# Routed experts of a two-layer transformer: the block loop pipelined one block deeper

## The chip, the cores and the metric

The kernel runs on one core of one Trainium2 chip. The metric is the device time of the whole program in microseconds (us); of the kernel before, three runs took 781.25, 782.66 and 784.82 us, median 782.66 us. The engines named below are TensorE (PE; its weight loads are PEld), VectorE (DVE), ScalarE (ACT), GpSimd (POOL) and SyncE (SP), which here only issues transfers. The profile is one execution, taken by the hardware profiler.

## The reference

The input x has 32 sequences of 128 tokens with 128 features; `ctx` holds 32 sequences of 77 context tokens. Two layers follow, each an attention to the context and a mixture of eight experts, of which every token uses two:

```
x = x + xattn0(layernorm(x), ctx)          # 16 heads, softmax over the 77 context tokens
x = x + moe0(layernorm(x))                 # 8 experts: (silu(x W1 + b1) * (x W2 + b2)) W3 + b3, 256 wide
x = x + xattn1(layernorm(x), ctx)          # linear attention: softmax over features of q and k
x = x + moe1(layernorm(x))                 # 8 experts: gelu(x W1 + b1) W2 + b2, 512 wide,
                                           # and the mean of 2 shared experts for every token
# top_k(router(x), 2) chooses the two experts; softmax of their two logits weighs them
```

All operands are 32-bit floats.

## The kernel before, in words

Layer 0 is attention (`attention0`), then the routed experts (`routed(0)`); layer 1 is attention with the shared experts woven into it (`attention1`), then `routed(1)`. Each routed stage is a loop over blocks of sorted rows, and the change concerns this loop alone.

While the attention of a layer runs, POOL scatters each token's normalized row twice (once for each chosen expert) into a table in HBM sorted by expert (`xs_sorted`, line 553). The table is then worked through in NB = 40 blocks for each layer, u = 0 to 39 in layer 0 and 40 to 79 in layer 1: 31 big ones of 256 rows (two tiles of 128) and 9 small ones of 128 rows, in the order ssss, then bbs five times, then big ones alone. Which expert a block belongs to is known only at run time: DVE computes it, and SP reads it from `e_i` to set the address of the transfer.

For each block the steps are these, in the names of the code:

- SP, `block_weights` (line 445): the expert's weights, 450 KB in layer 0 and 578 KB in layer 1, into one of NWB = 5 buffers `w_blk`. It waits until the outputs of block u - 5 have been added (`y_sum`). `block_rows` (line 457): the block's rows, 130 KB, into one of NXR = 8 buffers `xr`, AHEAD = 6 blocks in front. SP issues the transfers of all blocks in one order: weights of u + 5, rows of u + 6, weights of u + 6, and so on. In the preload it issues weights and rows in turn.
- PE, `turn_x` (through the helper at line 1355): transposes the rows into PSUM bank 6.
- DVE, `copy_x` (line 1011): copies bank 6 into `xT`, of which there are two.
- PE, `up` (through the helper at line 1352): four products with the weights into two of the banks 0 to 3 (a block uses banks 2k and 2k + 1 with k = u % 2). It waits for `xT_ready`, for the weights, and until the hidden values of block u - 2 have left these banks (`h_ready`).
- Layer 0: ACT applies silu (line 797, into `hg`), then DVE, `gated`, multiplies (line 1019, into `hT`). Layer 1: ACT applies gelu (line 801, into `hT`).
- PE, `down` (line 1640): the second product into bank 4 or 5.
- DVE, `outputs`: adds the bias (line 1028, this is `y_sum`) and scales by the gate (line 1032). POOL, `results` (line 626): scatters the tiles back to token order in HBM (`y_tok`), one indirect transfer for each tile.

PE's order in iteration u is turn_x(u + 1), up(u), down(u - 1). DVE's is copy_x(u + 1), outputs(u - 2), gated(u) in layer 0, and for the first 24 blocks of layer 0 a third of `context_soft`, which belongs to the attention of layer 1.

When all blocks are done, SP reads the token-ordered results back (line 498), DVE adds them to x (line 1058), and in layer 1 ACT stores x.

## Time and profile before

| what | value |
|---|---|
| three runs | 781.25, 782.66, 784.82 us, median 782.66 us |
| the profiled execution | 784.91 us, of which the span of its instructions is 782.9 us |
| PE busy | 688.5 us, 88% of the span |
| DVE, POOL, ACT busy | 465.7, 381.2, 327.3 us |
| mean granted TensorE clock | 0.942 of full speed |
| bytes moved | 91.34 MB, mean 117 GB/s |

The profile's page cuts the span into 40 slices of 19.6 us and gives the busy share of each engine in tenths. Layer 0's routed blocks lie in slices 15 to 21 (about 280 to 409 us), layer 1's in slices 32 to 39 (from 623 us; the last matmul ends at 765 us). A row of a timeline reads: start, duration, engine, line, operation, output <- inputs, shapes, how many are merged, and in brackets how long the engine had been idle and what ended that. "remote" as a releaser means that the profile could not say which instruction sent the signal. Ends of matmuls are modelled, so the time of a stage of PE is best read from start to start.

### The profile page before, as it was taken

The page shows a single profiled execution, that of the slowest core. Times are in us where ns is not written, and L with a number is a line of the kernel's source. Part 1 is how long each engine was busy: PE and PEld are TensorE (multiplying, and loading weights), DVE is VectorE, ACT ScalarE, POOL GpSimd, SP SyncE. Part 2 cuts the span into 40 slices and gives each one's busy share as a digit, 9 for nine tenths or more (in the row PEclk, how much of TensorE's full clock was granted, in tenths as well). Part 3 has the DMA queues.
Part 4 walks back from the last instruction along what each step waited for, and adds up shares of the span by engine and source line. Part 5 has one row for each costly group of instructions (what it writes and reads, how often), then busy time and mean ns, then how long its engine had stood idle before and what let it go on. Part 6 is the DMA issues. An engine that isn't in the chain of part 4 may idle for free.

```text
span 782.9 us, 15683 instructions
## 1 busy us (share of the span) xinstructions
PE 688.5 (88%) x5118; PEld 510.3 (65%) x5118; DVE 465.7 (59%) x1347; ACT 327.3 (42%) x689; POOL 381.2 (49%) x502
## 2 busy tenths in 40 slices
PE   4999999999898968889878799999999689999990
PEld 2666666566666657878766545555554389999990
DVE  2566877787677667676656667676653523324326
ACT  2344455445333232222212456667764244444440
POOL 5213176566537524555551365555555414454452
PEclk9999999999889789999997899999999979999996
DMA  6811111221101457776756000000000478877769
GB/s 164 258 12 10 10 28 26 30 30 25 32 12 35 126 166 237 215 225 204 212 165 173 0 18 21 28 29 21 24 28 27 123 234 258 270 238 246 227 196 285
DMA packets 102120, 91.34 MB, mean 117 GB/s; under 512 B 52953, under 2 KB 85849, under 8 KB 101721
## 3 DMA queue, kind: packets, MB, share of 16 engines
q1 hardware_dynamic: 86375, 68.80, 32.4%
q0 software_dynamic: 8640, 17.84, 6.4%
q10 hardware_dynamic: 7025, 3.70, 1.9%
q8 instruction: 42, 0.69, 0.4%
q14 instruction: 38, 0.30, 0.1%
HBM read 69.13 MB, written 22.72 MB: 117 GB/s over the span
## 4 chain that ended last, share of the span: by engine, by line
PE 53%; DVE 18%; issue 8%; DMA 5%; POOL 4%; ACT 4%; SPq 4%; another core or an unknown queue 3%; POOLq 0%; DVEq 0%; ACTq 0%
PE pair L1352 27%; PE pair L1640 10%; PE pair L1355 8%; DVE sm L1116 3%; DVE smax L1112 3%; POOL xs_sorted L553 2%; DMA xr<-xs_sorted 2%; PE pair L1458 2%; PE pair L1692 2%; PE pair L1473 2%; ACT xa L663 2%; DMA y_tok<-ysb,xr 1%; DMA xa<-y_tok 1%; DVE bns L1062 1%
## 5 line engine op out<-in xcount | busy, mean ns | idle before, releaser
L626 POOL DMA_INDIRECT y_tok<-ysb,xr x142 | 137.6, 969 | 145.5 <-DVE ysb L1032 116.3
L553 POOL DMA_INDIRECT xs_sorted<-xa,slot_i x128 | 130.2, 1017 | 93.5 <-DVE slot_i L939 59.0
L1352 PE MATMUL pair<-xT,w_all 128*128 128x256 f32 (+1 forms) x640 | 142.9, 369 | 0.0
L1640 PE MATMUL pair<-w_all,hT 128*128 128x128 f32 x852 | 110.8, 279 | 10.1 <-DVE hT L1019 10.0
L1352 PEld LDWEIGHTS pair<-xT,w_all 128*128 128x128 f32 x640 | 112.6, 201 | 10.4
L1640 PEld LDWEIGHTS pair<-w_all,hT 128*128 128x128 f32 x852 | 108.1, 195 | 15.1 <-issue 12.0
L801 ACT ACTIVATE hT<-pair,w_all 128x256 f32<-128x256 f32 (+1 forms) x160 | 62.0, 448 | 78.6 <-PE pair L1352 78.1
L1011 DVE COPY xT<-pair 128x256 f32<-128x256 f32 (+1 forms) x80 | 31.5, 394 | 104.9 <-PE pair L1355 88.7
L797 ACT ACTIVATE hg<-pair,w_all 128x256 f32<-128x256 f32 (+1 forms) x80 | 31.7, 447 | 93.5 <-PE pair L1352 68.3
L1112 DVE TENSOR_REDUCE smax<-pair 128x8 f32<-128x616 f32 x64 | 50.5, 788 | 33.2 <-PE pair L1352 32.8
L1352 PE MATMUL pair<-xeT_all,w_sh 128*128 128x512 f32 x128 | 69.2, 623 | 0.0
L818 ACT ACTIVATE hS<-pair,w_sh 128x512 f32<-128x512 f32 x64 | 43.9, 686 | 53.5 <-PE pair L1352 43.2
L1692 PE MATMUL pair<-hS,w_sh 128*128 128x512 f32 x128 | 65.4, 593 | 0.0
L1355 PEld LDWEIGHTS pair<-cst,sm 128*128 128x128 f32 x320 | 37.2, 151 | 26.4 <-issue 26.4
L1355 PE MATMUL pair<-cst,sm 128*128 128x128 f32 x320 | 52.8, 300 | 0.2 <-issue 0.2
L1116 DVE TENSOR_TENSOR sm<-pair,smax 128x616 f32<-128x616 f32 x64 | 51.2, 799 | 2.2
L1352 PE MATMUL pair<-hT,yS 32*128 32x308 f32 x192 | 41.8, 514 | 11.6 <-DVE sm L1116 10.0
L1355 PE MATMUL pair<-cst,xr 128*128 128x128 f32 x142 | 30.7, 288 | 18.7 <-DMA xr<-xs_sorted 7.0
L1019 DVE SCALAR_TENSOR_TENSOR hT<-pair,w_all,hg 128x256 f32<-128x256 f32 (+1 forms) x80 | 32.6, 448 | 24.2 <-remote 15.1
L701 ACT ACTIVATE wide<-pair 128x384 f32<-128x384 f32 x64 | 24.5, 434 | 44.5 <-PE pair L1355 44.5
L701 ACT ACTIVATE hS<-pair 128x384 f32<-128x384 f32 x64 | 24.6, 433 | 34.3 <-PE pair L1355 34.3
L1692 PEld LDWEIGHTS pair<-hS,w_sh 128*128 128x128 f32 x128 | 23.0, 190 | 23.7 <-issue 21.2
(194 smaller groups left out, 1100.5 us busy)
## 6 DMA issues: line engine op xcount, KB each, us to landing
w_all<-in_w SPq DMA_DIRECT2D x40, 578.0 KB
w_all<-in_w SPq DMA_DIRECT2D x40, 450.0 KB
xa<-y_tok SPq DMA_DIRECT2D x32, 256.0 KB, 5.6
xr<-xs_sorted SPq DMA_DIRECT2D x62, 130.0 KB
y_tok<-ysb,xr POOLq DMA_INDIRECT x142
xs_sorted<-xa,slot_i POOLq DMA_INDIRECT x128
out<-x_sb ACTq DMA_DIRECT2D x8, 256.0 KB, 3.1
xs_sorted<-in_pads SPq DMA_DIRECT2D x12, 130.0 KB, 4.3
```

The lines of the kernel that those rows point to most:

```text
L553: g.indirect_dma_start(xs_dram[l], bass.IndirectOffsetOnAxis(ap=slot_i[:, i:i + 1], axis=0), xa[:, GT * c + j // TOPK, j % TOPK, :], None) ...
L626: g.indirect_dma_start(y_dram[l], bass.IndirectOffsetOnAxis(ap=xr[u % NXR][:, t, P:P + 1].bitcast(I32), axis=0), ysb[u % NYB][:, t, :], None)\
L701: s_.activation(pT[T % 2][gr][:, 0:n], bank[2 + gr % 2][:, 0:n], ACT.Exp, scale=SCALE)\
L801: s_.activation(hT[k][:, c, 0:n], src, ACT.Gelu, bias=w[:, bcol + c:bcol + c + 1])\
L818: s_.activation(hS[i % 4][:], bank[4 + i % 2][:], ACT.Gelu, bias=w_sh[:, col:col + 1])\
L1019: v.scalar_tensor_tensor(hT[k][:, c, 0:n], chunk(bank[2 * k + 1], c, BLK)[:, 0:n], w[:, bcol + c:bcol + c + 1], hg[k][:, c, 0:n], ALU.add, ...
L1112: link(v.reduce_max(smax[ab][:].rearrange("q (b h) -> q b h", b=2), score(ab), AX.X))
L1116: v.tensor_tensor(sm[ab][:, 0:SPAN].rearrange("q (b h k) -> q b h k", b=2, k=NK), score(ab), smax[ab][:].rearrange("q (b h) -> q b h", b=2 ...
L1352: return mm(out_, l_, r_, start=True, stop=True)
L1355: return nc.tensor.transpose(out_, in_, ident)
L1640: last = mm(bank[4 + k][:, t * P:(t + 1) * P], hT[k][:, c, t * P:(t + 1) * P], chunk(w, nu + c, P), start=(c == 0), stop=(c == nc_ - 1))
L1692: mm(bank[6][:], w_sh[:, wd:wd + P], hS[i % 4][:], start=(c == 0), stop=(c == NC1S - 1))\
```

## The change

Buffers: six for weights instead of five, twelve for rows instead of eight, three each for `xT`, `hg`, `hT` instead of two. Rows are loaded 8 blocks ahead instead of 6. The room comes from `early`, one region that layer 0's attention uses first (`sm`, `kf4`, `rden`, `rdx`, `lent`) and the routed blocks afterwards. Rows are transposed two blocks ahead, into bank 6 or 7 in turn, and `down` runs two blocks back. On DVE `gated` comes one iteration later and stands before `outputs`, and `outputs` comes one later. Four row buffers count on the semaphores of the first inputs (`rows_in`), and one semaphore of ACT goes.

```diff
-NWB = 5
-NXR = 8
-AHEAD = NXR - 2
+NWB = 6
+NXR = 12
+AHEAD = 8
+DEEP = 3
...
-        w_all = sb("w_all", [P, NWB * WMAX])
-        w_blk = [w_all[:, i * WMAX:(i + 1) * WMAX] for i in range(NWB)]
+        early = sb("early", [P, 4300])
+        w_all = sb("w_all", [P, (NWB - 1) * WMAX])
+        w_blk = [w_all[:, i * WMAX:(i + 1) * WMAX] for i in range(NWB - 1)] + [early[:, 0:WMAX]]
...
+        def rows_in(u):
+
+            i = u % NXR
+            if i < 8:
+                return f"xr_in{i}", 16 * (u // NXR)
+            return f"x_in{i - 8}", 16 * (u // NXR + 1)
...
 (ACT, routed: up)
-                            after(act, S("h_ready"), NC0 * (u - 2) + c + 1)
-                            s_.activation(hg[k][:, c, 0:n], src, ACT.Silu, bias=w[:, bcol + c:bcol + c + 1])\
+                            after(act, S("h_ready"), NC0 * (u - DEEP) + c + 1)
+                            s_.activation(hg[u % DEEP][:, c, 0:n], src, ACT.Silu, bias=w[:, bcol + c:bcol + c + 1])\
...
 (DVE, routed)
                 def copy_x(u):
                     dve.wait_ge(S("xT_done"), u + 1)
-                    after(dve, S("up_done"), 2 * (u - 1))
+                    after(dve, S("up_done"), 2 * (u - DEEP + 1))
                     n = tiles_of(u) * P
-                    v.tensor_copy(xT[u % 2][:, 0:n], bank[6][:, 0:n]).then_inc(S("xT_ready"), 1)
+                    v.tensor_copy(xT[u % DEEP][:, 0:n], bank[6 + u % 2][:, 0:n]).then_inc(S("xT_ready"), 1)
...
                 copy_x(u0)
-                for u in range(u0, u1 + 2):
-                    if u + 1 < u1:
-                        copy_x(u + 1)
-                    if u >= u0 + 2:
-                        outputs(u - 2)
-                    if u < u1 and l == 0:
-                        gated(u)
+                copy_x(u0 + 1)
+                for u in range(u0, u1 + 3):
+                    if u + 2 < u1:
+                        copy_x(u + 2)
+                    if u0 < u <= u1 and l == 0:
+                        gated(u - 1)
+                    if u >= u0 + 3:
+                        outputs(u - 3)
...
 (PE, routed)
                 def turn_x(u):
-                    pe.wait_ge(S(f"xr_in{u % NXR}"), 16 * (u // NXR + 1))
-                    after(pe, S("xT_ready"), u)
+                    name, earlier = rows_in(u)
+                    pe.wait_ge(S(name), earlier + 16)
+                    after(pe, S("xT_ready"), u - 1)
                     for t in range(tiles_of(u)):
-                        last = turn(bank[6][:, t * P:(t + 1) * P], xr[u % NXR][:, t, 0:P])
+                        last = turn(bank[6 + u % 2][:, t * P:(t + 1) * P], xr[u % NXR][:, t, 0:P])
...
                 turn_x(u0)
-                for u in range(u0, u1 + 1):
-                    if u + 1 < u1:
-                        turn_x(u + 1)
+                if l == 1:
+                    pe.wait_ge(S("sx_added"), NGRP)
+                turn_x(u0 + 1)
+                for u in range(u0, u1 + 2):
+                    if u + 2 < u1:
+                        turn_x(u + 2)
                     if u < u1:
                         up(u)
-                    if u > u0:
-                        down(u - 1)
+                    if u > u0 + 1:
+                        down(u - 2)
```

The waits of `up` (`xT_ready` of u, the weights, `h_ready` of block u - 2) stay as they were.

PE, the start of layer 1's blocks. `cst,yS` is the last transpose of the shared experts, `cst,xr` is turn_x, `xT,w_all` is up, `w_all,hT` is down; in the changed kernel some buffers bear the name `early`. Before:

```order
L1355 MATMUL pair<-cst,yS 128x128 x4
L1355 MATMUL pair<-cst,xr 128x128 x2
L1352 MATMUL pair<-xT,w_all 128x128 x4
L1355 MATMUL pair<-cst,xr 128x128
L1352 MATMUL pair<-xT,w_all 128x128 x4
L1640 MATMUL pair<-w_all,hT 128x128 x4
L1355 MATMUL pair<-cst,xr 128x128
```

Changed:

```order
L1366 MATMUL pair<-cst,yS 128x128 x4
L1366 MATMUL pair<-cst,xr 128x128 x3
L1363 MATMUL pair<-xT,w_all 128x128 x4
L1366 MATMUL pair<-cst,xr 128x128
L1363 MATMUL pair<-early 128x128 x4
L1366 MATMUL pair<-cst,early 128x128 x2
L1363 MATMUL pair<-xT,w_all 128x128 x4
L1652 MATMUL pair<-w_all,hT 128x128 x4
```

Three blocks are transposed before the first up instead of two, and the first down comes after the third up instead of the second.

DVE, two blocks late in layer 0, where nothing else is woven in (`xT<-pair` is copy_x, `ysb` are the two operations of outputs, `hT<-pair,w_all,hg` is gated). Before:

```order
L1011 COPY xT<-pair 128x256
L1028 TENSOR_TENSOR ysb<-pair,w_all 128x256
L1032 TENSOR_TENSOR ysb<-ysb,xr 128x256
L1019 SCALAR_TENSOR_TENSOR hT<-pair,w_all,hg 128x256 x2
L1011 COPY xT<-pair 128x256
L1028 TENSOR_TENSOR ysb<-pair,w_all 128x256
```

Changed:

```order
L1021 COPY xT<-pair 128x256
L1029 SCALAR_TENSOR_TENSOR hT<-pair,w_all,hg 128x256 x2
L1038 TENSOR_TENSOR ysb<-pair,w_all 128x256
L1042 TENSOR_TENSOR ysb<-ysb,xr 128x256
L1021 COPY xT<-pair 128x256
L1029 SCALAR_TENSOR_TENSOR hT<-pair,w_all,hg 128x256 x2
```

The gated product now stands between the copy and the outputs of its iteration.

## Rows read from the trace of the kernel before

**Rows 1.** The page: its head, and granted clock in 40 slices.

```profile
span 782.9 us, 15683 instructions
...
PEclk9999999999889789999997899999999979999996
```

**Rows 2.** Busy time by stretch (busy us, instructions), then clock, DMA share, GB/s.

```profile
280.00:409.00 129.00, 111.58 (x677) 100.63 (x678) 87.26 (x229) 32.64 (x81) 65.41 (x68) 0.95 0.68 203
622.00:643.00 21.00, 15.24 (x89) 14.08 (x90) 4.79 (x16) 6.47 (x20) 2.97 (x4) 0.76 0.74 216
643.00:762.00 119.00, 119.00 (x848) 112.89 (x847) 39.29 (x107) 55.00 (x139) 60.43 (x63) 1.00 0.78 239
```

**Rows 3.** Waits, 265 to 420 us: who for whom, total, times, longest.

```profile
PE pair L1640 <- DVE hT L1019: 10.0, 5, 2.7
PE pair L1355 <- DVE xT L1011: 4.5, 4, 1.4
PE pair L1355 <- DMA xr<-xs_sorted: 2.4, 4, 1.6
```

**Rows 4.** Timeline of layer 0, one block and the stall behind it.

```profile
378.27 0.38 PE L1355 MATMUL pair<-cst,xr 128*128 128x128 f32 x2
...
381.11 0.38 PE L1355 MATMUL pair<-cst,xr 128*128 128x128 f32 x2
...
381.32 1.89 PE L1352 MATMUL pair<-xT,w_all 128*128 128x256 f32 x8
...
383.05 1.05 PE L1640 MATMUL pair<-w_all,hT 128*128 128x128 f32 x8
...
384.95 0.42 DVE L1011 COPY xT<-pair 128x256 f32<-128x256 f32 x1 [3.41 <-remote]
...
385.29 0.41 DVE L1028 TENSOR_TENSOR ysb<-pair,w_all 128x256 f32<-128x256 f32 x1
...
385.52 0.41 PE L1355 MATMUL pair<-cst,xr 128*128 128x128 f32 x2 [1.42 <-DVE xT L1011]
...
386.08 0.87 DVE L1019 SCALAR_TENSOR_TENSOR hT<-pair,w_all,hg 128x256 f32<-128x256 f32 x2
```

**Rows 5.** Timeline of PE in the middle of layer 1's blocks.

```profile
718.70 0.38 PE L1355 MATMUL pair<-cst,xr 128*128 128x128 f32 x2
...
720.64 1.95 PE L1640 MATMUL pair<-w_all,hT 128*128 128x128 f32 x16
722.43 0.38 PE L1355 MATMUL pair<-cst,xr 128*128 128x128 f32 x2
```

**Rows 6.** Timeline of SP's queue at the start of layer 1's blocks.

```profile
627.17 0.33 SPq L457 DMA_DIRECT2D xr<-xs_sorted  x1
628.27 0.33 SPq L445 DMA_DIRECT2D w_all<-in_w  x1
629.91 0.33 SPq L457 DMA_DIRECT2D xr<-xs_sorted  x1
...
632.68 1.99 SPq L457 DMA_DIRECT2D xr<-xs_sorted  x2
```

**Rows 7.** Timeline of PE there.

```profile
626.77 0.48 PE L1355 MATMUL pair<-cst,xr 128*128 128x128 f32 x1 [2.62 <-DMA xr<-xs_sorted]
...
629.56 0.48 PE L1355 MATMUL pair<-cst,xr 128*128 128x128 f32 x1 [0.60 <-DMA xr<-xs_sorted]
...
641.98 0.33 PE L1355 MATMUL pair<-cst,xr 128*128 128x128 f32 x1 [1.31 <-DMA xr<-xs_sorted]
642.15 1.90 PE L1352 MATMUL pair<-xT,w_all 128*128 128x256 f32 x8
```

**Rows 8.** Timeline of the end: the last two down products, POOL's scatters of blocks 78 and 79.

```profile
761.47 3.73 PE L1640 MATMUL pair<-w_all,hT 128*128 128x128 f32 x32
...
765.33 0.96 POOL L626 DMA_INDIRECT y_tok<-ysb,xr  x1 [2.00 <-DVE ysb L1032]
...
767.87 0.96 POOL L626 DMA_INDIRECT y_tok<-ysb,xr  x1 [0.30 <-issue]
```

More of the change, by code:

```diff
@@ L262, in build @@
         smax = [sb(f"smax{i}", [P, 2 * HG]) for i in range(2)]
-        sm = [sb(f"sm{i}", [P, NCK * P]) for i in range(2)]
-        kf4 = sb("kf4", [P, GT * NK])
-        rden = sb("rden", [P, P])
-        rdx = sb("rdx", [P, GT * P])
+        sm = [early[:, i * NCK * P:(i + 1) * NCK * P] for i in range(2)]
+        kf4 = early[:, 3328:3328 + GT * NK]
+        rden = early[:, 4148:4148 + P]
+        rdx = early[:, 3636:3636 + GT * P]
         cxm = sb("cxm", [P, 3, GT * H])
-        lent = [sb(f"lent{i}", [P, 1024])[:] for i in range(2)]
+        lent = [early[:, 1280 + i * 1024:1280 + (i + 1) * 1024] for i in range(2)]
         lg = sb("lg", [P, NT, E])
@@ L309, in build @@
         below = sb("below", [1, len(SETS), NYB * NQ])
[L312 to L315 removed]
+        xr = [sb(f"xr{i}", [P, 2, ROW]) for i in range(8)] + \
+             [early[:, 3072 + i * 2 * ROW:3072 + (i + 1) * 2 * ROW].rearrange("p (t d) -> p t d", t=2) for i in range(NXR - 8)]
+        xT = [sb(f"xT{i}", [P, BLK]) for i in range(2)] + [early[:, 2816:2816 + BLK]]
+        hg = [sb(f"hg{i}", [P, NC0, BLK]) for i in range(2)] + [early[:, 2304:2304 + NC0 * BLK].rearrange("p (c n) -> p c n", c=NC0)]
+        hT = [sb(f"hT{i}", [P, NC1, BLK]) for i in range(2)] + [early[:, 1280:1280 + NC1 * BLK].rearrange("p (c n) -> p c n", c=NC1)]
         ysb = [sb(f"ysb{i}", [P, 2, P]) for i in range(NYB)]
@@ L655, in _ @@
             act.wait_ge(S("pool_const"), 8)
-            s_.activation(table[:], ones_row[:, 0:1], ACT.Exp).then_inc(S("table"), 1)
+            s_.activation(table[:], ones_row[:, 0:1], ACT.Exp)
             act.wait_ge(S("head_in"), 16)
@@ L1017, in gated @@
                         dve.wait_ge(S("up_done"), 2 * u + 2)
-                        after(dve, S("down_done"), u - 1)
-                        v.scalar_tensor_tensor(hT[k][:, c, 0:n], chunk(bank[2 * k + 1], c, BLK)[:, 0:n],
-                                               w[:, bcol + c:bcol + c + 1], hg[k][:, c, 0:n], ALU.add, ALU.mult)\
+                        after(dve, S("down_done"), u - DEEP + 1)
+                        v.scalar_tensor_tensor(hT[u % DEEP][:, c, 0:n], chunk(bank[2 * k + 1], c, BLK)[:, 0:n],
+                                               w[:, bcol + c:bcol + c + 1], hg[u % DEEP][:, c, 0:n], ALU.add, ALU.mult)\
                             .then_inc(S("h_ready"), 1)
@@ L1629, in up @@
                     for c in range(nu):
-                        last = one(chunk(bank[2 * k + c // 2], c % 2, BLK)[:, 0:n], chunk(w, c, P), xT[k][:, 0:n])
+                        last = one(chunk(bank[2 * k + c // 2], c % 2, BLK)[:, 0:n], chunk(w, c, P), xT[u % DEEP][:, 0:n])
                         if c % 2 == 1:
@@ L1639, in down @@
                         for c in range(nc_):
-                            last = mm(bank[4 + k][:, t * P:(t + 1) * P], hT[k][:, c, t * P:(t + 1) * P],
+                            last = mm(bank[4 + u % 2][:, t * P:(t + 1) * P], hT[u % DEEP][:, c, t * P:(t + 1) * P],
                                       chunk(w, nu + c, P), start=(c == 0), stop=(c == nc_ - 1))
```

12 lines of the change are left out of this document (4 added, 8 removed).

## The prediction

> **What bounds the kernel now.** I read the page first: 782.9 us of span with a clock that falls below full speed in some slices [rows 1]. The change acts only in the two loops over routed blocks, so I cut these out by stretches of time. Layer 0's blocks take 129 us, in which PE is busy 111.6 us; the DMA engines are busy 68%, DVE 87.3 us [rows 2]. Layer 1's blocks fall in two parts: a start of 21 us with PE busy for only 15.2 us at a mean clock of 0.76, and then 119 us in which PE is busy for all 119.0 us at full clock [rows 2]. So in the body of layer 1 PE itself is the bound. There a block takes 722.43 - 718.70 = 3.73 us from turn to turn with nothing in between [rows 5], and no amount of buffering shortens it. What more buffering can win lies in layer 0 and at the two starts.
>
> In layer 0 the list of waits says what PE lacks: 10.0 us in five waits before `down` for the gated product, 4.5 us in four waits before `turn_x` for the copy of the previous block, 2.4 us in four for rows from HBM [rows 3]. A block that runs without a gap takes 381.11 - 378.27 = 2.84 us: turn 0.21, up 1.73 (383.05 - 381.32), down the remaining 0.90 [rows 4].
>
> The timeline of one stall shows what kind of wait it is. PE's transpose at 381.11 is over by 381.5, DVE has nothing to do, and yet its copy starts only at 384.95, after 3.41 us of idle time whose releaser the profile can't name. Meanwhile PE goes on with up and down until about 383.95 (381.11 + 2.84), then runs dry; the next transpose starts at 385.52, 1.57 us late [rows 4]. So signals from PE reach DVE late now and then, by more than the loop has in hand. The rows don't say why. The question is how much delay the new loop bears, and at which signal.
>
> **The change part by part.** The number of instructions on PE, DVE, ACT, POOL and SP is the same for every block; only order and distance change. So each term is a change of idle time on PE, or at the ends.
>
> *Waits for the gated product.* Before, gated(u) is needed by down(u), which follows down(u - 1), turn_x and up(u + 1) after up(u): 0.90 + 0.21 + 1.73 = 2.84 us of cover. After, down(u) is two blocks back, but up(u + 2) writes the banks that gated(u) reads and still waits for it. It comes 0.90 + 0.21 = 1.11 us later than the place where PE waited before. Against that, DVE now has the copy of block u + 3 in front of gated(u), 0.42 us [rows 4]. Net 0.69 us for each of the five waits: 3.4 us gained. Bounds: all 10.0 us gained (no late signal finds the loop short), and nothing gained. I take 3.4, since the bank rule is in the code and the distances are from rows.
>
> *Waits for the copy.* Before, a late signal of the transpose costs from the moment PE runs dry (2.84 us after the transpose started) to release + copy. After, PE goes on into the next transpose, 0.21 us more, and then stands before up(u + 1), which needs gated(u - 1), which on DVE stands behind the late copy. So the price becomes release + copy + gated, and gated takes 0.87 us [rows 4]: 0.87 - 0.21 = 0.66 us more for each of four waits, 2.6 us lost. Bounds: 4.5 us gained if these delays no longer matter, 2.6 us lost. I take the loss, as the stall in [rows 4] begins at exactly this signal.
>
> *Lead of the transfers.* SP may load weights when outputs of an old block are added. Before, outputs(u) runs in DVE's iteration u + 2 and the weights go to block u + 5; after, in iteration u + 3 for block u + 6: three iterations both times. Rows likewise, u + 6 turned in iteration u + 5, and u + 8 turned in iteration u + 6. The sixth and the twelve buffers only carry the deeper loop. But outputs now stand behind gated, 0.87 us later in their iteration [rows 4], so every transfer has 0.87 us less. PE waited for rows four times in layer 0 [rows 3]; the loss lies between nothing and, if one block in three of 40 falls short, 13 x 0.87 = 11.3 us. I take one such delay, 0.9 us lost, nearest to the small wait of 2.4 us that the trace has.
>
> *The start of layer 1.* PE transposes two ahead, so up(40) waits for the rows of block 42 instead of 41: these are in at 629.56 instead of 626.77 [rows 7]. The start is paced by SP, which spends 629.91 - 627.17 = 2.74 us for a pair of rows and weights, of which 1.10 us goes from rows to weights and 1.64 from weights to rows [rows 6]. Rows of blocks 44 and 45 were issued back to back from 632.68; now the sixth weights go between them, and rows of 46 and 47 follow at once, by my count issued at 632.68, 635.4, 637.1 and 638.7 with weights at 633.8. With 629.56 - 627.17 = 2.4 us from issue to transpose the rows of 47 are in at about 641.1. In between PE does up(43), down(41), up(44), down(42) and is at up(45) at about 642.9, where before it was at 642.15 [rows 7]; but before, down(43) was done by then, a small one of half of 1.79 us (720.64 to 722.43 [rows 5]). So 0.75 + 0.9 = 1.6 us lost, which the saturated body can't give back. Bounds: 0.9 (only the deferred product) and 3.0 (the rows of 46 take the 4.3 us that they took before). The new wait on `sx_added` has nothing behind it but this loop and is met before the rows of 41 arrive. The start of layer 0 is like it but waits longer for other things; by the same count its first big blocks come out even, 0.
>
> *The ends.* The last three down products of a layer now run back to back. In layer 1 a down takes 1.79 us [rows 5], but POOL takes 767.87 - 765.33 = 2.54 us to scatter a block [rows 8]. Before, two ran back to back and block 79's scatter waited on POOL for block 78; now 77, 78 and 79 queue up: 2.54 - 1.79 = 0.75 us later. Bounds 0 and 1.5. In layer 0 the same happens, but down(38) now covers part of the wait before down(39), which is among the five.
>
> The sum against the profiled execution: 784.91 - 3.4 + 2.6 + 0.9 + 1.6 + 0.75 = 787.4 us. The median of the runs is 2.25 us under the profiled time, so 785.1 us is what I forecast for the median, 2.4 us (0.3%) over 782.66. A difference below 0.5% (3.9 us) can't be told from no change here.
>
> **The rivals.**
>
> *The delays are absorbed.* The waits of PE for DVE in layer 0, 14.5 us [rows 3], mostly vanish. For it: the gaps come again and again, and the loop has one buffer more of each kind. The Trainium skill speaks for this: its page "Perfetto Trace Analysis", section on identifying performance opportunities, says that the same gap repeating on the engine that should be full can mean that there are too few buffers for the next tile. By that rule alone the 14.5 us would go. Against it stands that banks 0 to 3 still hold only two blocks, and that the copy now carries the gated product behind it. With all gone and start and end as above: 784.91 - 14.5 + 1.6 + 0.75 = 772.8, in the median 770.5; with two thirds gone, 775.3. Faster.
>
> *The lead runs short.* Outputs 0.87 us later shift weights and rows of every block. When PE runs at 2.84 us a block, three iterations are 8.5 us; from this about 1.1 us went before for turn, copy and first output, and 2.0 go now, so 6.5 us remain for SP, transfer and signal. If that fails for a third of the blocks: 784.91 - 3.4 + 2.6 + 11.3 + 1.6 + 0.75 = 797.8, median 795.5. For it: the DMA engines already move 239 GB/s in layer 1 and 203 in layer 0 [rows 2], with rows waited for four times. Against it: the waits for rows are 2.4 us in all. It decides once rows land less than 0.9 us before their turn. Slower; with half of it, 790.
>
> *Nothing moves.* The bank rule caps the loop at two blocks as before and the late signals find the same gap; only start and end count: 784.91 + 2.4, median 785.0. This gives the same number as the forecast and goes with it.
>
> **How the numbers follow.** Forecast with its neighbour "nothing moves": 0.40. Absorbed, wholly or in part: 0.31. Lead short, or late signals that cost more than I count: 0.29. The forecast's own range is 781 to 789: of it about a tenth lies over 786.6, and the two rivals reach into the band within 0.5% with a few in a hundred each. That gives faster by over 0.5% 0.31, within 0.5% 0.36, slower 0.33. For 8 in 10, I go down to 771, where all of the 14.5 us is gone, and up to 794, near the short lead in full.
>
> **What would show it.** In layer 0 the group of waits of `down` for the gated product should be gone and PE should wait before `up` instead, for the gated product, in total some 7 us of the old and 4 x 2.2 us for late copies. In a stall like that of [rows 4], DVE should run copy, gated, outputs in a row and PE start up after the gated product. Layer 0's blocks should take 128 to 131 us. In layer 1 the first up should start near 629.8 on the old clock of the trace instead of 627.04, and the body should still be 3.73 us a block with PE full. POOL's last scatter should start about 0.75 us later after the last down. The forecast is wrong if layer 0's blocks take under 124 us (delays absorbed), or if waits for `xr<-xs_sorted` or for weights grow beyond 6 us there (lead short).

## The result: 1.1% slower, and the profile after

The changed kernel took 790.78 us (median of 20 runs) beside 781.58 us for the kernel before (20 runs on the same chip): 1.0106 of its time, 95% interval 1.0085 to 1.0127, or some 8.3 us more. That ratio leaves out one slow run of the changed kernel (796.1 us), and the medians alone lie 9.2 us apart. The forecast was 0.3% more, no change that can be told.

The page and the stretches of the changed kernel, which answer to [rows 1, 2] (layer 0's blocks, the start of layer 1's, their body; us busy, then clock, DMA share, GB/s):

```profile
span 789.1 us, 15679 instructions
...
PEclk8699999998998779999996799999999879999995
...
279.80:406.30 126.50, 110.70 (x673) 98.95 (x672) 84.76 (x226) 32.19 (x81) 64.47 (x65) 0.97 0.68 207
626.50:648.00 21.50, 15.18 (x85) 13.65 (x86) 4.20 (x14) 7.40 (x22) 2.41 (x3) 0.68 0.74 221
648.00:769.90 121.90, 121.81 (x876) 115.63 (x874) 40.17 (x110) 55.32 (x138) 61.83 (x65) 1.00 0.79 242
```

The body of layer 1 is full as before. PE's waits from 265 to 420 us, which answer to [rows 3] (L1363 is the up products, L1366 the transposes, L1652 the down products):

```profile
PE pair L1363 <- DVE hT L1029: 8.7, 8, 2.2
...
PE pair L1366 <- DMA xr<-xs_sorted: 2.3, 4, 1.3
PE pair L1366 <- DMA early<-xs_sorted: 2.1, 4, 1.0
PE pair L1652 <- DVE ysb L1038: 2.0, 2, 1.5
...
PE pair L1366 <- DVE xT L1021: 0.3, 1, 0.3
```

No wait of a down product for the gated product is left; it is the up products that wait for it, 8.7 us where the old two groups had 14.5. Waits for rows rose from 2.4 to 4.4 us, and two waits for a bank of outputs came to 2.0. A stall like that of [rows 4]:

```profile
352.52 0.42 DVE L1021 COPY xT<-pair 128x256 f32<-128x256 f32 x1 [2.82 <-remote]
...
352.73 0.44 PE L1366 MATMUL pair<-cst,xr 128*128 128x128 f32 x2 [1.28 <-DMA xr<-xs_sorted]
352.86 0.87 DVE L1029 SCALAR_TENSOR_TENSOR hT<-pair,w_all,hg 128x256 f32<-128x256 f32 x2
353.64 0.41 DVE L1038 TENSOR_TENSOR ysb<-pair,w_all 128x256 f32<-128x256 f32 x1
353.87 1.97 PE L1363 MATMUL pair<-early,w_all 128*128 128x256 f32 x8 [0.70 <-DVE hT L1029]
```

Copy, gated product and outputs stand in a row behind the late signal, and the up product starts when the gated product is done, as forecast.

Layer 1's start and PE's block there, and the last scatter, which answer to [rows 5 to 8]:

```profile
626.54 0.45 PE L1366 MATMUL pair<-cst,xr 128*128 128x128 f32 x1 [2.14 <-issue]
630.42 0.45 PE L1366 MATMUL pair<-cst,xr 128*128 128x128 f32 x1 [3.43 <-DMA xr<-xs_sorted]
632.57 0.47 PE L1366 MATMUL pair<-cst,xr 128*128 128x128 f32 x1 [1.70 <-DMA xr<-xs_sorted]
632.84 1.49 PE L1363 MATMUL pair<-xT,w_all 128*128 128x128 f32 x6
...
721.73 0.38 PE L1366 MATMUL pair<-cst,early 128*128 128x128 f32 x2
...
725.46 0.38 PE L1366 MATMUL pair<-cst,early 128*128 128x128 f32 x2
...
766.07 3.74 PE L1652 MATMUL pair<-w_all,hT 128*128 128x128 f32 x32
...
773.07 1.03 POOL L636 DMA_INDIRECT y_tok<-ysb,xr  x1 [0.30 <-issue]
```

and the first transpose of the kernel before:

```profile
623.85 0.30 PE L1355 MATMUL pair<-cst,xr 128*128 128x128 f32 x1 [1.22 <-issue]
```

From first transpose to first up product it was 627.04 - 623.85 = 3.19 us and is 632.84 - 626.54 = 6.30. A block is still 725.46 - 721.73 = 3.73 us. The last block's scatter (the first of its two transfers) begins 773.07 - 769.81 = 3.26 us behind the last down product (2.66 before).

Cut at these marks, in us of the two profiled executions:

| stretch | before | after | difference |
|---|---|---|---|
| to layer 0's first up product | 280.44 | 279.87 | -0.6 |
| layer 0's blocks | 127.7 | 126.3 | -1.4 |
| last down product to layer 1's first transpose | 215.7 | 220.3 | +4.6 |
| first transpose to first up product | 3.2 | 6.3 | +3.1 |
| layer 1's blocks | 138.2 | 137.0 | -1.2 |
| last down product to the end | 17.7 | 19.3 | +1.6 |

That is the 6.2 us between the two spans. The largest term lies in a stretch whose own order of work the change does not touch.

### The profile page after: what moved, and what is told of

Read it like the earlier page. It is cut to its first block, busy times and chain, and to the rows that moved or that the text cites. A ratio compares the mean times of both kernels' runs of the same rounds, so it can differ in the third digit from the quotient of the medians.

```text
span 789.1 us, 15679 instructions
## 1 busy us (share of the span) xinstructions
PE 689.3 (87%) x5118; PEld 508.4 (64%) x5118; DVE 465.0 (59%) x1347; ACT 327.9 (42%) x689; POOL 382.1 (48%) x502
## 4 chain that ended last, share of the span: by engine, by line
PE 53%; DVE 17%; issue 10%; SPq 6%; DMA 5%; POOL 5%; ACT 4%; POOLq 0%; DVEq 0%; ACTq 0%
PE pair L1363 28%; PE pair L1652 10%; PE pair L1366 8%; DVE early L1127 3%; DVE smax L1123 3%; POOL xs_sorted L563 2%; PE pair L1469 2%; PE pair L1707 2%; PE pair L1484 2%; DMA early<-xs_sorted 2%; ACT xa L673 2%; SPq L461 1%; DMA y_tok<-ysb,xr 1%; SPq L454 1%; DVE bns L1073 1%
## 5 line engine op out<-in xcount | busy, mean ns | idle before, releaser
L636 POOL DMA_INDIRECT y_tok<-ysb,xr x97 | 95.0, 979 | 110.3 <-DVE ysb L1042 90.6
L1363 PE MATMUL pair<-xT,w_all 128*128 128x256 f32 (+1 forms) x432 | 92.4, 360 | 0.0
L1363 PEld LDWEIGHTS pair<-xT,w_all 128*128 128x128 f32 x432 | 73.8, 201 | 6.2 <-issue 0.2
L1652 PEld LDWEIGHTS pair<-w_all,hT 128*128 128x128 f32 x552 | 70.2, 194 | 3.0 <-DVE ysb L1038 0.6
L1652 PE MATMUL pair<-w_all,hT 128*128 128x128 f32 x552 | 71.1, 277 | 0.4 <-DVE ysb L1038 0.4
L1363 PE MATMUL pair<-xeT_all,w_sh 128*128 128x512 f32 x128 | 69.1, 623 | 0.0
L1366 PE MATMUL pair<-cst,early 128*128 128x128 f32 x397 | 66.0, 296 | 3.2 <-DMA early<-xs_sorted 2.7
L1366 PEld LDWEIGHTS pair<-cst,early 128*128 128x128 f32 x397 | 46.1, 149 | 31.1 <-issue 27.2
L811 ACT ACTIVATE hT<-pair,w_all 128x256 f32<-128x256 f32 (+1 forms) x108 | 41.4, 439 | 58.7 <-PE pair L1363 56.0
L636 POOL DMA_INDIRECT y_tok<-ysb,early x45 | 43.9, 975 | 36.9 <-DVE ysb L1042 28.3
L1127 DVE TENSOR_TENSOR early<-pair,smax 128x616 f32<-128x616 f32 x64 | 51.2, 799 | 2.2
L1363 PE MATMUL pair<-hT,yS 32*128 32x308 f32 x192 | 41.5, 509 | 11.6 <-DVE early L1127 9.9
```

What stands on the lines that cost most here:

```text
L636: g.indirect_dma_start(y_dram[l], bass.IndirectOffsetOnAxis(ap=xr[u % NXR][:, t, P:P + 1].bitcast(I32), axis=0), ysb[u % NYB][:, t, :], None)\
L811: s_.activation(hT[u % DEEP][:, c, 0:n], src, ACT.Gelu, bias=w[:, bcol + c:bcol + c + 1])\
L1127: v.tensor_tensor(sm[ab][:, 0:SPAN].rearrange("q (b h k) -> q b h k", b=2, k=NK), score(ab), smax[ab][:].rearrange("q (b h) -> q b h", b=2 ...
L1363: return mm(out_, l_, r_, start=True, stop=True)
L1366: return nc.tensor.transpose(out_, in_, ident)
L1652: last = mm(bank[4 + u % 2][:, t * P:(t + 1) * P], hT[u % DEEP][:, c, t * P:(t + 1) * P], chunk(w, nu + c, P), start=(c == 0), stop=(c == ...
```

## The experiments

Every variant is the changed kernel with an edit; each is compared with the kernel before on its own chip. There are two sorts of chip here: the kernel before takes 750 to 752 us on some, called fast, and 782 to 786 on others, called slow, among them that of the prediction. In both loops the depth is written as `TA[l]` (transposes ahead) and `DB[l]` (down products back). The loop of PE:

```
+TA, DB = (2, 2), (2, 2)
-    if u + 2 < u1: turn_x(u + 2)
+    if u + TA[l] < u1: turn_x(u + TA[l])
-    if u > u0 + 1: down(u - 2)
+    if u >= u0 + DB[l]: down(u - DB[l])
```

and that of DVE, where the place of the gated product hangs on `TA`:

```
     if u + TA[l] < u1: copy_x(u + TA[l])
     if TA[l] == 2 and u0 < u <= u1 and l == 0: gated(u - 1)
     if u >= u0 + DB[l] + 1: outputs(u - DB[l] - 1)
     if TA[l] == 1 and u < u1 and l == 0: gated(u)
```

So in layer 0 a variant with `TA` of 1 also has each gated product one iteration earlier and behind the outputs. No run moves the transposes alone and leaves the gated product where it was.

**Which part costs?** `TA, DB = (2, 1), (2, 1)` (layer 1 old), then `(1, 2), (1, 2)` (layer 0 old), then `(1, 1), (1, 1)` (buffers alone).

> The changed kernel with layer 1's block loop at its old depth (transposes one block ahead, down products one back, outputs two back); layer 0 keeps the new depth, and all the new buffers stay. My theory from the two traces: layer 1's depth costs 3.5 us (first transpose to first up 3.1 us longer, body 1.2 us shorter, tail after the last down product 1.6 us longer), so this kernel should run about 787.3 us where the changed one ran 790.8 (before: 781.6). Rival 1, that all of the loss comes out of layer 0's end and the buffers: 790.8, no change. Rival 2, that layer 1's depth is all of the loss: 781.6.

> The changed kernel with layer 0's block loop at its old depth; layer 1 keeps the new depth, and all the new buffers stay. My theory: layer 0's depth gains 2.0 us up to its last down product (start 0.6, blocks 1.4) and loses 4.65 us between there and layer 1's first transpose, net 2.6 us lost, so about 788.2 us. If the stretch between the layers is only chance of the one profiled execution, layer 0's depth is a gain of 2 us and this kernel is slower than the changed one: 792.8. If layer 0's depth is all of the loss: 781.6.

> The changed kernel with both block loops at the old depth: what is left of the change is the sixth weight buffer, the twelve row buffers with rows issued eight ahead, the shared region for attention's and the loop's buffers, and the copy of the transpose in three buffers. My theory, in which depth alone costs: within 1 us of the kernel before, 781 to 782.5. Rival, that the buffers or the earlier loads cost (the start of a layer with more loads queued, the region shared by both): 785 to 791, as slow as the changed kernel. A gain, if rows that arrive earlier spare the 2.4 us of waits for rows: 779.

Measured, on a fast chip: layer 1 old 1.006 (1.0037 to 1.0084), layer 0 old 1.0008 (0.9979 to 1.0038), buffers alone 0.996 (0.9941 to 0.998). So the buffers gain 3 us, the new depth in layer 0 costs 1.0% (7.5 us) and in layer 1 0.5% (3.6 us). I had given layer 0 the smaller share, 2.6 us; the sizes were off, that of layer 1 was right, and the rival that layer 0 is only chance fell.

The traces of these kernels, with those of the kernel before and the changed one on another fast chip (next experiment), cut at the same marks (us, one execution each):

| stretch | before | buffers alone | layer 0 deep (layer 1 old) | layer 1 deep (layer 0 old) | changed |
|---|---|---|---|---|---|
| to layer 0's first up product | 265.4 | 266.0 | 268.1 | 265.9 | 267.9 |
| layer 0's blocks | 109.3 | 107.0 | 111.4 | 105.9 | 111.7 |
| last down product to layer 1's first transpose | 216.2 | 218.7 | 220.5 | 219.0 | 220.6 |
| first transpose to first up product | 1.0 | 1.8 | 1.7 | 4.4 | 4.0 |
| layer 1's blocks | 136.8 | 137.5 | 137.7 | 136.7 | 136.6 |
| last down product to the end | 17.5 | 17.5 | 18.1 | 19.3 | 19.5 |
| at half clock, first 90 us behind layer 0 | 13.7 | 23.9 | 23.9 | 23.9 | 23.9 |

Two things stand out. On a fast chip the new depth of layer 0 loses most in its own blocks, 4.4 us beside the buffers alone, and only 1.8 us behind them. And the stretch between the layers is already 2.5 us longer in the two kernels whose layer 0 has the old depth, with ten more microseconds at half clock. These 2.5 us are not the depth's; whether they come from the buffers or from chance in a single execution, no run tells.

**The level, the whole change and the lead of rows.** The kernel before and the changed one again, then two edits of it.

> The kernel before, for a trace from the same chip as the variants (its level differs from chip to chip: 781.6 us beside the changed kernel, 752.2 beside the first four variants). With the kernel of the buffers alone layer 0's blocks took 107 us without the bursts of late signals that the first trace had (127.7 us). If the bursts belong to the chip and not to the kernel, this trace has layer 0's blocks at 107 to 112 us; if the new buffers took them away, at 125 to 129 us.

> The changed kernel, on the chip of the variants. From the three variants (buffers alone 0.996, new depth in layer 1 alone 1.0008, in layer 0 alone 1.006) the parts add up to 0.996 + 0.0048 + 0.010 = 1.011 of the time before, 760.4 us at 752.2, if they are independent. If the two depths hinder each other or hide each other: 1.016 or 1.006.

```
+    if u >= u0 + 3: outputs(u - 3)
     if u0 < u <= u1 and l == 0: gated(u - 1)
-    if u >= u0 + 3: outputs(u - 3)
```

> The changed kernel with the outputs of block u-3 in front of the gated product of block u-1 on DVE, as before the change. Theory: in layer 0 every load of weights and rows is released by an addition of outputs that now stands some 0.8 us later in its iteration (1.4 us behind the last down product instead of 0.6), PE waits 5.0 us for rows, and this lead is what the new depth loses: the waits for rows fall to under 2 us and the time by 2 to 4 us against the changed kernel, 1.006 to 1.008 of before. Rival, that the gated product is the tighter need (PE's next up product waits for it): the time rises by 1 to 3 us, 1.012 to 1.015.

```
-AHEAD = 8
+AHEAD = 10
```

> The changed kernel with rows issued ten blocks ahead instead of eight (the twelve buffers allow it). Theory of the short lead: with two more blocks of lead PE's waits for rows in layer 0 vanish (5.0 us in nine waits with the new depth in layer 0), the time falls by 3 to 5 us against the changed kernel, 1.005 to 1.007 of before; layer 1's start is unchanged, as rows of its first three blocks are issued at the same time. Rival, that weights are what is short or DVE's order costs: no change, 1.011. Rival, that more rows issued at a layer's start delay the weights: 1.012 to 1.014.

Measured on one fast chip: before 748.1 us in the one execution with a trace, 750.5 in the median of 13 runs, which the ratios use; changed 1.0155 (1.0113 to 1.0198); outputs first 1.0135 (1.0089 to 1.0181); rows ten ahead 1.0101 (1.0068 to 1.0135). The changed kernel came out above the 1.011 to which the parts add up, near the 1.016 of parts that hinder each other, though the parts were measured on another chip. Outputs first missed its 1.006 to 1.008 and fell into the rival's range. Rows ten ahead missed its ratio, but is 4.3 us faster than the changed kernel, of the 3 to 5 expected. Layer 0's blocks took 109.3 us in the kernel before, with no late signals. In that stage DVE stood idle for over 1.5 us before a signal that the profile can't name ten times in the kernel before on the first chip (1.8 to 3.8 us each), and not once here. The buffers alone and the changed kernel have no such case on fast chips either, so the late signals go with the chip. PE's waits in layer 0 there, of the kernel before, the changed one and with rows ten ahead:

```profile
PE pair L1355 <- DMA xr<-xs_sorted: 4.9, 6, 1.7
```

```profile
PE pair L1366 <- DMA early<-xs_sorted: 3.0, 5, 1.0
PE pair L1366 <- DMA xr<-xs_sorted: 1.9, 3, 1.1
```

```profile
PE pair L1371 <- DMA xr<-xs_sorted: 1.7, 2, 1.0
```

With no late signals PE waits for rows instead, and two more blocks of lead take 3.2 of 4.9 us away; the blocks went from 111.7 to 108.3 us, the median from 762.7 to 758.4. The kernel of buffers alone has no such wait and blocks of 107.0 us. So the changed kernel gives away the lead that its buffers hold. The first blocks stayed slow: from the first up product to the fourth it is 6.7 us before, 8.4 changed and 9.1 with rows ten ahead. PE's idle time in it is 1.02, 1.05 and 1.69 us. In the changed kernel PE stands before a transpose whose rows SP has only just issued, in front of an up product that is ready, and the clock is at half for longer: until 276.5 us, 8.6 us behind the first up product, where it was until 268.3, 2.9 us behind it. The third up product, before and changed:

```profile
269.24 1.12 PE L1352 MATMUL pair<-xT,w_all 128*128 128x128 f32 x8
```

```profile
272.78 0.69 PE L1366 MATMUL pair<-cst,xr 128*128 128x128 f32 x2 [1.05 <-DMA xr<-xs_sorted]
273.26 1.92 PE L1363 MATMUL pair<-early,w_all 128*128 128x128 f32 x8
```

**Between the layers.** The chain of waits behind layer 0's last down product, in the kernel before, in the changed one and with outputs first, all on that fast chip (the last down product ends at 374.7, 379.5 and 379.4 us):

```profile
373.39 5.42 DMA y_tok<-ysb,xr
...
378.88 3.99 DMA xa<-y_tok
382.96 0.70 DVE x_sb L1058
...
390.63 2.09 PE pair L1352 x8
```

```profile
381.07 5.33 DMA y_tok<-ysb,xr
...
386.46 2.79 DMA xa<-y_tok
...
389.35 0.70 DVE x_sb L1069
...
397.01 5.51 PE pair L1363 x24
402.52 0.87 PE pair L1366 x4
...
404.06 6.66 PE pair L1363 x14
```

```profile
378.95 5.08 DMA y_tok<-ysb,xr
...
384.10 2.88 DMA xa<-y_tok
...
387.07 0.70 DVE x_sb L1074
...
394.74 5.51 PE pair L1368 x24
```

Read how far each is behind its last down product. The combination of results (DVE x_sb) comes at 8.3, 9.8 and 7.6 us, since more scatters queue up on POOL. In all three chains the load waits for the sixth scatter from the end; it begins 2.6 us before the last down product ends, 0.3 us after it and 1.7 us before it. The last block's scatter begins 2.5, 5.3 and 3.3 us behind. Then PE has its first big piece. In the changed kernel it runs at half clock (1.2 GHz of 2.4):

```profile
392.00:410.00 18.00, 15.13 (x53) 11.99 (x54) 11.83 (x30) 6.40 (x12) 2.95 (x7) 0.53 0.20 50
```

The clock was full up to 392.6, PE idle for most of 387.5 to 392, and half from 392.6 to 409.6. In the kernel before it was half from 387.7 to 394.6 only. The stretch took 216.2, 220.6 and 217.5 us: outputs first gave 3.0 us back with as much half clock as the changed kernel (23.9 us in the 90 us from there in both). Two tries at the clock and one at the scatters follow. `keep_clock(n, b)` issues n matmuls of 128x512 whose result nothing uses:

```
                 for g in range(NGRP - 2): context_product(g)
+            keep_clock(3, 3)                 # fill_mid
...
                     if live(u): input_turned(u)
+                    if u == 0: keep_clock(1, 3)
```

> The changed kernel with four matmuls added that compute nothing used: three after the context products at the end of layer 0 and one behind attention 1's first four transposes, both where PE stood idle in the trace (420.4 to 422.3 us and 423.4 to 424.1 us). My theory: PE's clock was granted at half from 421.7 to 435.4 us after this idle time, and that is what costs 2.5 to 4.6 us between the layers; with PE kept busy the stretch at half clock moves or shrinks and the time falls by 2 to 4.5 us, to 786.3 to 788.8. Rival, that the lag comes from the data (late results, POOL's queue of scatters) and not from the clock: no gain, or 0.5 to 1 us lost, as the added matmuls stand in the way: 790.8 to 791.8.

```
-                    keep_clock(3, 3)
+                    keep_clock(12, 3)        # fill_early, in front of the wait
```

> The changed kernel with nine more matmuls of 0.43 us that compute nothing used, put in front of the context product of group 5 at layer 0's end, where PE stands idle for 4 to 5 us waiting for DVE (the four of the earlier try stood behind this wait, ran at half clock and delayed attention 1's first transposes by 4 us). Theory of the clock: PE's clock stays at full through this wait, the half clock of 17 us after it shrinks to under 10, the 24 matmuls behind the first transposes take 2.1 us instead of 5.5, and the stretch between the layers shrinks by 2 to 3 us: 1.3 to 3 us faster than the changed kernel. Rival, that the clock falls all the same or that nothing on the path is PE's: no change.

```
+def back(l, k): return 1 if l == 0 and k >= NB - 3 else DB[l]   # after_drain: in place of DB[l]
```

> The changed kernel, with the down products of layer 0's last three blocks one block back instead of two (layer 0 otherwise, and layer 1, as changed). Theory: of the 4.4 to 4.7 us that the changed kernel loses between layer 0's last down product and layer 1's first transpose, about 2 come from three scatters that queue up on POOL (last scatter 5.3 to 5.5 us behind the last down product, 2.5 to 3.3 before) and so from results that are combined later. With this drain the last scatter begins 2.5 to 3.3 us behind, the stretch shrinks from 220.5 to about 218.5 us, and the time falls by 1.5 to 3 us against the changed kernel (1.0106 and 1.0155 of before on two chips). Rival, that the stretch is longer for the clock alone: stretch and time unchanged.

The first filler gave 1.0121 (1.0087 to 1.0155), no gain to be told from the changed kernel, which was not run on that chip: it ran at half clock in front of attention 1's first transposes. `fill_early` gave 1.0091 (1.0059 to 1.0124), `after_drain` on the same chip 1.0132 (1.0095 to 1.0169). The drain failed at its aim: the last scatter still began 5.0 us behind, the stretch stayed at 220.2 us, so it says nothing on the scatters. In `fill_early` the clock held through the wait, the stretch was 218.4 us, and 13.7 us of the 90 were at half (27.3 in `after_drain`):

```profile
381.00:394.00 13.00, 12.83 (x45) 6.81 (x44) 4.47 (x16) 1.67 (x5) 4.03 (x7) 1.00 0.94 261
394.00:411.00 17.00, 13.18 (x69) 9.44 (x70) 14.25 (x41) 5.93 (x10) 2.54 (x6) 0.90 0.00 0
```

I had mis-sized the filler: each call is two instructions of 0.43 us, so that nine more are 7.8 us, longer than the wait of 4.8 us:

```profile
382.14 10.46 PE L1368 MATMUL pair<-cst 128*128 128x512 f32 x24
```

It shortened the stretch by 2 us beside `after_drain` although it held up the results' third combination by 2. The times of the two kernels overlap.

**Transposes or down products?** `DB = (1, 1)` alone, and `TA = (1, 1)` alone, on a slow chip like that of the prediction.

> The changed kernel with the transposes two blocks ahead in both layers but the down products one block back, as before (buffers and all else as changed). Theory, from the traces of one chip: transposes two ahead cost only at the start of a layer, where PE must wait for one more block of rows before it may begin the first up products: 2.0 us more idle time between the first three up products of layer 0 and 2.6 to 3.0 us from first transpose to first up product in layer 1. Over the buffers alone (0.996 of before) that is 4.8 us, 1.002. Rival, that the transposes' place is harmless and the down products are all of it: 0.996. Rival, that it is all of the loss: 1.015.

> The changed kernel with the down products two blocks back but the transposes one ahead. Theory: down products two back cost only at the end of a layer, where three blocks' scatters queue up on POOL: the last scatter begins 5.3 us behind the last down product in layer 0 instead of 2.5 (results are loaded and combined that much later), and layer 1's tail is 1.2 to 1.8 us longer: 4.3 us over the buffers alone, 1.002 of before. The first up products of a layer come as early as before the change. Rival, that the short lead of rows (3.3 us, gone with rows ten ahead) belongs to the down products and not to the pair of both: 1.006.

> Both loops at the old depth with the new buffers, and rows issued ten blocks ahead instead of eight. The buffers alone took away the waits for rows that the kernel before has in layer 0 (4.9 us in six waits) and gave 0.996. If no wait for rows is left there, two more blocks of lead change nothing: 0.995 to 0.997. If more rows at a layer's start get in the way of the first weights: 0.998 to 1.0.

Measured: transposes alone 1.0073 (1.0047 to 1.0099), down products alone 1.0009 (0.9981 to 1.0038), buffers with rows ten ahead 0.9976 (0.9947 to 1.0005). The transposes, in layer 0 together with the later gated product, are the larger loss. Transposes alone fell between the expected 1.002 and the rival's 1.015, down products alone met the expected 1.002, and the buffers with rows ten ahead came out just above their expected 0.995 to 0.997, not told from no change. PE's waits in layer 0, transposes alone, then down products alone:

```profile
PE pair L1657 <- DVE hT L1031: 10.3, 7, 3.1
PE pair L1657 <- DVE early L1031: 8.4, 7, 2.2
```

```profile
PE pair L1368 <- DVE early L1023: 7.3, 7, 1.4
PE pair L1368 <- issue: 3.6, 7, 1.2
```

With transposes alone, DVE forms the gated product one iteration later, behind the copy of a transpose that PE begins only one up product earlier, and the down products wait 18.7 us for it where [rows 3] has 10.0; the blocks take 130.1 us (127.7). That argues for the place of the gated product as the cause in layer 0; transposes two ahead with the gated product in its old place were not tried. Down products two back do what deeper buffering should: 120.6 us, 7.1 less. Both kernels also hold the new buffers, and the buffers with ten rows ahead have 125.2 us on this chip: measured from there the one loses 4.9 us and the other gains 4.6, with a lead that differs. The layer's end takes it back: 221.0 us to layer 1's first transpose instead of 215.7 (218.4 with the buffers and ten rows ahead), and layer 1 and the tail take 2.1 us more. From first transpose to first up product the transposes take 6.2 us, the down products 3.5.

**Old depth at the ends, and a version that keeps the gain.** Three kernels: depth changed inside a layer, and layer 0's down products two back but drained, without and with the filler.

```
+def ta(k): return 1 if k < 4 else 2          # ramp, with AHEAD = 10, outputs first
+def db(k): return 1 if k < 4 or k >= NB - 3 else 2
```

> The changed kernel with the old depth in the first four and the last three blocks of each layer and the new depth between them, rows ten ahead, outputs in front of the gated product on DVE. If the new depth costs only at the starts and ends of the layers and through the lead of rows, this kernel is as fast as the buffers alone: 0.995 to 0.998 of before. If the deeper loop also costs in the body, 1.002 or more; if it gains there, under 0.994.

> Only layer 0 with the down products two blocks back (but one back in its last three blocks), transposes one ahead in both layers, layer 1 at its old depth, buffers as changed. On the chip with bursts of late signals the down products two back shortened layer 0's blocks by 7.1 us (120.6 us for 127.7) and lost 5.3 us of it in the stretch behind and some more in layer 1. With the loss at the end taken away and layer 1 as before: 0.990 to 0.995 of before. If layer 0's gain only moves the wait to the results (they are paced by something that does not move with the blocks): 0.998 to 1.001.

> The same kernel as the one with layer 0's down products two back and drained, plus the nine matmuls in front of the context product of group 5. Theory of the clock: 2 to 3 us faster than that kernel, 0.987 to 0.992 of before. Rival: the same time.

`ramp` took 1.008 (1.0046 to 1.0114), not told from the changed kernel, where 0.995 to 0.998 was expected. Its ends were mended: 214.6 us between the layers where the changed kernel has 220.3 and buffers with ten rows ahead 218.4, and 3.6 us to layer 1's first up product instead of 6.3. But layer 0's blocks took 128.6 us and layer 1's 142.7, where the other kernels on that chip have 136.6 to 139.2: what the ends gave back the loops lost, and why is not shown. `down0_drain` took 0.9998 (0.9977 to 1.0019) and `down0_fill` 0.9977 (0.9955 to 1.0), both on a fast chip, where there are no late signals for the depth to absorb; the intervals overlap. Both missed their 0.990 to 0.995 and 0.987 to 0.992: layer 0's blocks took 106.3 and 107.3 us, as the buffers alone.

**All mends at once, and the best candidate.**

> The changed kernel with three of its losses mended at once: outputs in front of the gated product on DVE (0.2% less by itself), rows ten ahead (0.54% less), nine matmuls that hold the clock (0.2 to 0.3% less). If these are separate causes they add up: 1.0155 - 0.0020 - 0.0054 - 0.0025 = 1.0056 of before on a chip of the fast sort. What is then left, 4.2 us of 750, should be what the new depth costs at the starts of the layers (2.0 us in layer 0, 2.6 to 3.0 in layer 1) and in the tail. If they mend the same thing: 1.010.

> Both loops at the old depth with the new buffers (0.996 of before), plus the nine matmuls that keep PE busy in front of the context product of group 5. They took 1.2 us from the stretch between the layers beside a kernel with layer 0 deep in the down products (0.9998 to 0.9977) and 2.1 us at the changed kernel. Here the clock was at half for 17 us behind that wait too. Theory of the clock: 0.994 of before. Rival, that on the old depth the matmuls are in the way: 0.996 to 0.998.

Both were measured on a slow chip: 1.0178 (1.0146 to 1.0211), above the changed kernel's 1.0106 on another slow chip, and 1.0089 (1.0057 to 1.0122), slower than before. Both expectations failed. The second kernel has rows eight ahead, and no run of the buffers alone on a slow chip stands beside it. In it the clock was at half before the filler began (windows, then PE's timeline):

```profile
408.00:424.00 16.00, 14.33 (x53) 12.00 (x54) 9.01 (x26) 1.16 (x3) 6.10 (x9) 0.50 0.84 244
```

```profile
411.71 7.25 PE L1368 MATMUL pair<-kvm_all,wide 77*128 77x129 f32 x32 [0.52 <-DVE ysb L1040]
...
420.48 12.50 PE L1368 MATMUL pair<-cst 128*128 128x512 f32 x24
432.81 1.06 PE L1368 MATMUL pair<-kvm_all,hS 77*128 77x129 f32 x8
```

The filler took 12.5 us, and the stretch 223.1 us where buffers with rows ten ahead have 218.4 on another slow chip; but layer 0's blocks, which hold no filler, are 4.0 us longer too (129.2 and 125.2), so the loss is not the filler's alone. In `after_mended` layer 0's blocks took 129.3 us and the last scatter came 5.0 us behind the last down product of layer 1. So the mends did not add up there. Each was found on a fast chip. That they mend something which costs nothing on a slow one is only a guess, as none was run alone there. No version was shown to beat the kernel before on both sorts. Buffers alone did on a fast chip (0.996), and with rows ten ahead the slow chip shows 0.9976, not told from no change.

## Why the prediction was wrong

- **Layer 0's end, the step that failed.** "In layer 0 the same happens, but down(38) now covers part of the wait before down(39)": I put it at nothing. The stretch from there to layer 1 is +4.6 us here and +4.4 on the fast chip. I had looked at where PE ends, not at where the results end, and I had taken the stretch behind for untouched. Only a part of it is the depth: on fast chips it is 220.5 and 220.6 us where the same buffers with layer 0 at the old depth have 218.7 and 219.0, so 1.5 to 1.9 us. On slow chips single traces scatter more: 220.3 and 221.0 us with layer 0's down products two back, and 213.9 (transposes alone), 215.7 (before) and 218.4 (buffers, rows ten ahead) with them one back. There POOL's queue moves the results' combination; outputs first took 3.0 us off this stretch with as much half clock, in one trace each. The other 2.5 us appear at the old depth too, on the fast chip with 23.9 us at half clock for 13.7, and the prediction had no term for them either. Their cause is open. The times of outputs first and of the filler agree in sign on fast chips, but their intervals overlap, and the kernel with the filler lost on a slow chip. The Trainium skill says in "TensorE: Matmul & The Clock Gate", Part 1, that for modeling the penalty of the clock's ramp is under 1% of a typical kernel's span and should not be fitted to a count of cold matmuls. It speaks of the ramp at a kernel's start. One half-clock stretch here is worth at most some 2.5 us of 790, by an estimate from the traces with 216.2 and 218.7 us between the layers, which is under that 1%, but not small beside a loss of 8.3 us.
- **Start of layer 0, "come out even, 0".** From the first up product to the fourth it is 5.5 us before and 6.6 changed in this trace, 6.7 and 8.4 on the fast chip: wrong by 1.1 and 1.7 us, with one down product less done by then. A transpose two ahead makes a ready up product wait for rows still to be issued, as in layer 1, and the clock stays at half for longer behind it.
- **Start of layer 1, 1.6 us.** Right place: 3.1 to the first up product less 1.2 in the blocks is 1.9. The first up product came 6.3 us behind the first transpose, where the sign of the forecast (629.8 for 627.04) asks for 6.0. By time alone, the new depth in layer 1 costs 3.6 us on the fast chip, with the tail.
- **Tail, 0.75 us.** The last scatter moved by 3.26 - 2.66 = 0.6 as said, the whole tail by 1.6.
- **Waits for the gated product, -3.4, and for the copy, +2.6.** The sign of the sum held (blocks -1.4), but it hid two opposite parts. Down products two back shorten the blocks by 7.1 us, transposes two ahead with the later gated product lengthen them by 2.4; from the buffers with ten rows ahead it is 4.6 and 4.9. Taken apart, the sum would have said which half to drop.
- **Lead of transfers, 0.9 us.** As far as the slow chip's trace goes, 2.4 to 4.4 us of waits for rows; where PE isn't held up by late signals, rows ten ahead gave 0.54%, 4 us. The rival "the lead runs short" named 790 as its price with half of it; that this is the time measured is luck, as its own sign, over 6 us of waits for rows in layer 0, did not show.
- **The rival of absorbed delays**, and with it the rule of "Perfetto Trace Analysis" in the Trainium skill that repeating gaps can mean too few buffers, was right for half the change at most: layer 0's blocks shrank by up to 7.1 us with down products two back. It was wrong for the whole: the 14.5 us of waits did not vanish with everything deeper, 8.7 us came back in front of the up products.
- **The signs.** Neither sign of being wrong fired (layer 0's blocks 126.3 us, not under 124; waits for rows 4.4 us, not over 6), and the order of copy, gated product and outputs, the 3.73 us a block and the last scatter came as said. The waits before the up products came to 8.7 us where some 16 were forecast, and layer 0's blocks stayed under the forecast 128 to 131. No sign looked at the stretch between the layers.

What stays open: whether the 2.5 us between the layers at the old depth are the buffers' or chance, and how the depth's 1.5 to 1.9 us divide; whether layer 0's blocks lose by the transposes or by the later gated product; why some chips give late signals; and where the 3 us come from that buffers alone gain, beyond the waits for rows. The 6.2 us of the stretches are one execution each, the 8.3 us a ratio over many.

## What to carry to other kernels

A deeper software pipeline has a price at each start and each end of the loop; count it to where the results are used, on every engine behind the loop (here POOL's scatters), not only to where PE stops. Deepen one side at a time: here down products later shortened the blocks on the chip with late signals and gained nothing without them, while transposes earlier made PE wait for rows that no ready product needed. When a reordering on one engine drags another along (the gated product here), move them in separate runs. Filler costs what it outlasts its wait by, and double where the clock has fallen: six of its instructions took 2.74 us at full and 5.14 us at half clock in `fill_mid`.

## What the hardware showed that I had not expected

- The same kernel took 750 to 752 us in three groups of runs and 782 to 786 in three others, each group on one chip. Layer 0's blocks are 109.3 us on one and 127.7 on another, and the size of a change's effect may differ with it: changed kernel 1.0155 (1.0113 to 1.0198) and 1.0106 (1.0085 to 1.0127), whose intervals just overlap.
- The half-clock stretch behind an idle PE at layer 0's end lasted 7 us in the kernel before and 17 in the changed one on the same chip; the buffers alone had 17 us too, with a stretch of 218.7 us for 216.2, though nothing in the loops' order had changed.
